# x normed by features on GpSimd from a second copy, another order of VectorE, and a last batch ended in halves

## The chip, the cores and the metric

One core of a Trainium2 chip runs the program. The metric is device microseconds of one execution, the median of the runs of a kernel. The engines are TensorE (PE in the profile; PEld is its weight load), VectorE (DVE), ScalarE (ACT), GpSimd (POOL) and SyncE (SP, which here only issues DMAs).

## The reference

For each of 16 batches of 512 tokens with 128 features:

```
n   = gamma * x / |x| * sqrt(128)                    # rms norm
q,k,v = n @ w_q * 0.25, n @ w_k, n @ w_v             # 8 heads of 16
phi(u) = [1, u, u_i * u_j / sqrt(2)]                 # second order Taylor features
att = phi(q) @ (phi(k)^T v) / max(phi(q) . sum phi(k), 1e-5)
x1  = layernorm(x + att @ w_out)
h   = silu(x1 @ w1 * s1) * (x1 @ w2 * s2)            # 128 -> 512
h   = gelu(h @ h1 * hs1); h = gelu(h @ h2 * hs2)     # 512 -> 512, exact gelu
out = layernorm(x1 + h @ w3 * s3)                    # 512 -> 128
```

All is float32. The kernel keeps the accuracy by splitting each activation into a rounded high part (type fp32r) and the rest, and multiplying each by the weights.

## The kernel before

Every engine has its own program, written out by hand; semaphores order them. The work is a pipeline over batches in steps t = 0 to 18: step t does the FRONT of batch t (norm of x, projections, phi(k), state, sums for phi(q)), the MIDDLE of batch t - 1 (state applied to phi(q), attention, projection, x1), the FFN of batch t - 2 and the TAIL of batch t - 3 (last layer norm, store). Steps 0 and 1 are mostly written out by themselves, steps 3 to 14 run in a loop of two steps a turn, and steps 15 to 18 are peeled. `B` is 16, `P` 128, `N` 512, `NT` and `KT` 4.

PSUM is two sets of four banks. `RING` lists in PE's order what is written into the attention's four banks (`ring`), `FPS` the same for the feed-forward part (`fps`). A write waits until the reader of the bank's last content has released it (`bank_wait`, `ring_free`, `f_free`).

x comes once per batch, tokens on partitions, into one of two buffers `x_b` (SP L277). ACT squares it (`square`, L629), DVE sums the squares (`sum_squares`, L829, L833), POOL takes the power -0.5 (L1080) and scales x (L1085, tile `xn`), all in the step before the batch's FRONT. PE transposes `xn` (`transpose_x`, L309) into the ring; ACT copies it rounded (`x_hi`, L639) and DVE subtracts (`x_lo`, L844). Then PE projects k and v in four products of tokens (`project_kv`, L322) and q (`project_q`, L329). ACT copies k and v out (`copy_kv`, L633), DVE makes the products of k (`phi_k_main`, L257), POOL the small features (`k_small`, L1099 to L1108); `copy_q` and `q_lo` (L852, L856) split q. `sums_of_q` and `rest_of_q` (L348, L355) make sums that ACT squares (`square_sums`, L660; `square_rest`). `state` (L368) is 64 small products. In the next step the state is transposed (L378, L385) and applied (L398, L407), `normalise` divides on DVE, `project_out` (L415) projects, and DVE adds x (`sum_x1`, L889), takes the variance and scales (`norm_scale`, L882); PE transposes x1 (L423), and ACT and DVE split it (L670, `x1_lo` L923).

The feed-forward products are pairs, high (L431) and low part (L434). `silu`, `gate_mult`, `gate_hi`, `gate_lo` (L696, L930, L701, L936) make the gate. `gelu` on ACT writes the rounded part (L709) and the exact one over the bank (L711), and `gelu_tile` on DVE (L944) subtracts. `copy_y` (L716), `transpose_y` (L476), `sum_z` (L907), POOL's power (L1122), `norm_scale` into `o_b` and the store (L282) end a batch.

`keep_busy` (L586) is a product on ones whose result nobody reads. `weights_low_bits` (L680) finds whether the weights have low bits that rounding would lose; after step 1 PE branches on the result.

## Time and profile before

| | |
|---|---|
| median of 3 runs | 564.23 us (562.71 to 565.49) |
| the profiled execution | 565.74 us, its span 563.9 us |
| busy share PE, DVE, ACT, POOL | 97%, 81%, 82%, 28% |
| share of the chain that ended last | PE 89%, issue 4%, ACT 2%, DVE 2% |
| products of the feed-forward part (L431, L434) in that chain | 28% and 27% |

Times in the rows are us from the start of the span. A busy PE row can hold pipelined products: starts tell more than durations. The granted clock of PE (PEclk) has two levels here, 1.2 and 2.4 GHz, 0.5 and 1.0 in the rows. The idle time in brackets is what came before the operation on its engine, with what ended it.

### The profile page before, as it was taken

What the parts mean: (1) busy time and instruction counts of PE and PEld (TensorE: products, weight loads), DVE (VectorE), ACT (ScalarE), POOL (GpSimd) and SP (SyncE); (2) the same over time, 40 slices, a digit from 0 to 9 for tenths busy, and PEclk for the clock granted to TensorE, in tenths of its full rate; (3) what the DMA queues carried; (4) which work ended last, traced back from release to release, by engine and by line L of the source; (5) the groups of instructions that cost most, each with busy time, mean ns of one, the idle gap of its engine ahead of it and who ended that gap; (6) DMA issues with size and microseconds to landing.
All of it is one profiled execution on the core that took longest, in us unless ns stands there. A gap on an engine that the chain in (4) does not pass through costs nothing.

```text
span 563.9 us, 11483 instructions
## 1 busy us (share of the span) xinstructions
PE 545.4 (97%) x3608; PEld 410.3 (73%) x3608; DVE 457.1 (81%) x982; ACT 460.5 (82%) x954; POOL 159.5 (28%) x246
## 2 busy tenths in 40 slices
PE   7879999999999999999999999999999999999994
PEld 3446877878687787868778786877878787786772
DVE  5776769888787988878798887879888787968764
ACT  4757797988979798897979889797988979787773
POOL 3541414223151422314142222414222241400000
PEclk9799999999999999999999999999999999999998
DMA  8000000000000000000000000000100000000000
GB/s 274 18 22 2 19 2 2 20 19 20 20 19 19 0 19 19 19 19 19 19 0 19 18 19 19 19 19 0 29 8 19 19 19 19 1 19 1 20 1 37
DMA packets 7366, 12.25 MB, mean 22 GB/s; under 512 B 816, under 2 KB 1840, under 8 KB 7344
## 3 DMA queue, kind: packets, MB, share of 16 engines
q1 hardware_dynamic: 7056, 11.86, 6.6%
q8 instruction: 13, 0.21, 0.2%
q10 hardware_dynamic: 288, 0.10, 0.1%
q14 instruction: 9, 0.07, 0.0%
HBM read 7.77 MB, written 4.19 MB: 21 GB/s over the span
## 4 chain that ended last, share of the span: by engine, by line
PE 89%; issue 4%; ACT 2%; DVE 2%; POOL 1%; DMA 1%; SPq 0%; POOLq 0%; DVEq 0%
PE fps L431 28%; PE fps L434 27%; PE ring L368 7%; PE ring L398 5%; PE ring L348 5%; PE ring L322 4%; PE ring L407 3%; PE ring L415 2%; PE ring L329 2%; PE fps L476 1%; PE fps L423 1%; PE ring L309 1%; PE ring L355 1%; DMA w_raw<-in_w 1%; PE ring L378 1%
## 5 line engine op out<-in xcount | busy, mean ns | idle before, releaser
L431 PE MATMUL fps<-hid_hi,w_hi 128*128 128x512 f32 x576 | 229.7, 399 | 0.0
L434 PE MATMUL fps<-hid_lo,w_hi 128*128 128x512 f32 x576 | 226.9, 394 | 1.3 <-DVE hid_lo L944 0.9
L709 ACT ACTIVATE hid_hi<-fps,col 128x512 fp32r<-128x512 f32 x128 | 90.3, 705 | 54.1 <-PE fps L434 54.1
L431 PEld LDWEIGHTS fps<-hid_hi,w_hi 128*128 128x128 f32 x576 | 108.3, 188 | 25.4 <-issue 3.4
L434 PEld LDWEIGHTS fps<-hid_lo,w_hi 128*128 128x128 f32 x576 | 108.3, 188 | 25.0 <-DVE hid_lo L944 2.2
L944 DVE TENSOR_TENSOR hid_lo<-fps,hid_hi 128x512 fp32r<-128x512 f32 x128 | 88.2, 690 | 32.4 <-ACT fps L711 30.8
L711 ACT ACTIVATE fps<-fps,col 128x512 f32<-128x512 f32 x128 | 86.6, 677 | 0.0
L660 ACT ACTIVATE phiT<-ring 128x512 f32<-128x512 f32 x127 | 77.2, 636 | 5.1 <-PE ring L348 4.0
L930 DVE SCALAR_TENSOR_TENSOR h<-fps,col,gate_zo 128x512 f32<-128x512 f32 x64 | 47.8, 748 | 38.7 <-ACT gate_zo L696 34.5
L257 DVE TENSOR_TENSOR phi_k<-phi_k 128x896 f32<-128x896 f32 x64 | 69.1, 1085 | 0.2 <-ACT v_one L633 0.2
L348 PE MATMUL ring<-qT,sel 128*128 128x512 f32 x128 | 52.9, 417 | 3.5 <-ACT v_one L633 2.0
L431 PE MATMUL fps<-x1T_hi,w_hi 128*128 128x512 f32 x128 | 52.5, 411 | 1.5 <-DVE x1T_lo L923 1.5
L1099 POOL TENSOR_TENSOR k_half<-v_one,const 128x16 f32<-128x16 f32 x32 | 14.6, 456 | 130.4 <-ACT v_one L633 128.7
L434 PE MATMUL fps<-x1T_lo,w_hi 128*128 128x512 f32 x128 | 51.0, 398 | 0.0
L701 ACT ACTIVATE hid_hi<-h 128x512 fp32r<-128x512 f32 x64 | 42.8, 668 | 9.1 <-DVE h L930 9.1
L1080 POOL TENSOR_TENSOR rn<-ssc,const 128x4 f32<-128x4 f32 x16 | 16.3, 1016 | 116.0 <-DVE ssc L833 115.8
L696 ACT ACTIVATE gate_zo<-fps,col 128x512 f32<-128x512 f32 x64 | 45.9, 717 | 1.9 <-PE fps L434 1.8
L936 DVE TENSOR_TENSOR hid_lo<-h,hid_hi 128x512 fp32r<-128x512 f32 x64 | 43.8, 684 | 1.8 <-ACT hid_hi L701 0.2
L689 ACT ACT_TABLE_LOAD x33 | 42.3, 1283 | 2.2 <-PEq L1187 1.7
L368 PE MATMUL ring<-phi_k,v_one 128*32 128x153 f32 x1024 | 38.6, 305 | 0.4 <-ACT phiT L660 0.4
L368 PEld LDWEIGHTS ring<-phi_k,v_one 128*32 128x32 f32 x1024 | 32.6, 114 | 7.2 <-issue 4.8
L1122 POOL TENSOR_TENSOR zrstd<-zveps,const 128x4 f32<-128x4 f32 x16 | 16.1, 1009 | 70.2 <-DVE zveps L918 70.2
(100 smaller groups left out, 902.3 us busy)
## 6 DMA issues: line engine op xcount, KB each, us to landing
x_b<-in_x SPq DMA_DIRECT2D x16, 256.0 KB, 2.6
out<-gate_zo SPq DMA_DIRECT2D x16, 256.0 KB, 2.0
w_raw<-in_h SPq DMA_DIRECT2D x2, 1024.0 KB, 9.4
w_raw<-in_w SPq DMA_DIRECT2D x3, 256.0 KB, 4.6
sel_raw<-in_sel SPq DMA_DIRECT2D x1, 320.0 KB, 6.0
w_qkv_raw<-in_w_kv SPq DMA_DIRECT2D x1, 128.0 KB, 2.8
const<-in_consts ACTq DMA_DIRECT2D x1, 92.0 KB, 3.0
w_qkv_raw<-in_w_q SPq DMA_DIRECT2D x1, 64.0 KB, 2.8
```

Source lines behind the costliest of these rows:

```text
L257: return eng.tensor_tensor(out, fixed, moved, ALU.mult)
L348: nc.tensor.matmul(ring[:, bank_of(RING, f"sq{f}"), :], sel[:, l * P:(l + 1) * P], qT[g][:, :], start=True, stop=True).then_inc(ring_full, 1)
L368: mm = nc.tensor.matmul(ring[32 * hh:32 * hh + 32, bank, g * FEAT:(g + 1) * FEAT], v_one[:, j, 4 * g + hh, :], phi_k[:, j, 4 * g + hh, 0:F ...
L431: nc.tensor.matmul(fps[:, bank, :], w[:, o:o + P], hi, start=start, stop=False)
L434: return nc.tensor.matmul(fps[:, bank, :], w[:, o:o + P], lo, start=False, stop=stop)
L660: nc.scalar.activation(phiT[:, f, :], ring[:, bank, :], ACT.Square).then_inc(ring_free[bank], 1)
L696: nc.scalar.activation(gate[:, m % 2, :], fps[:, bank_of(FPS, f"a{m}"), :], ACT.Silu, scale=s1_c[:, m:m + 1]).then_inc(f_free[bank_of(FPS, ...
L709: nc.scalar.activation(hid[1 - layer][0][:, m, :], fps[:, bank, :], ACT.Gelu, scale=scale)\
L711: nc.scalar.activation(fps[:, bank, :], fps[:, bank, :], ACT.Gelu, scale=scale)\
L930: nc.vector.scalar_tensor_tensor(out=h32[:, m, :], in0=fps[:, bank_of(FPS, b), :], scalar=s2_c[:, m:m + 1], in1=gate[:, m % 2, :], op0=ALU ...
L936: nc.vector.tensor_tensor(hid[0][1][:, m, :], h32[:, m, :], hid[0][0][:, m, :].bitcast(F32), ALU.subtract).then_inc(split_ready, 1)
L944: nc.vector.tensor_tensor(lo, fps[:, bank, :], hi.bitcast(F32), ALU.subtract)\
```

## The change

The host hands over x twice, once as before and once with features first (`xT`). From step 2 on PE no longer transposes x. SP loads x by tokens (`x_nrm`) for the squares, x by features (`x_cols`) for the products, and x again for the residual (`x_res`). POOL's powers (`norm_of_x`) go as 512 numbers to DRAM (`rn_rows`) and come back as a row on every partition (`rn_row`, `spread_norms`). In the batch's own step POOL multiplies `x_cols` by it (`normed_cols`), ACT makes the rounded copy from that (`scaled_hi`), and POOL subtracts in DVE's place; PE waits for that (`x_lo_ready`). Batches 0 and 1 keep the transposes.

ACT squares the next batch's x ahead of the gelus of layer 2, not between those of layer 3. DVE sums the squares behind `sum_z`, splits `q_lo` around `sum_x1`, takes the variance (`var_of_x1`) behind the last gelu tile of layer 2 and makes all products of k after it.

At the start, `weights_low_bits(1)` goes behind the first step's squares; all but three of the sums of batch 1 move ahead of PE's branch; PE gets more `keep_busy`; the load of the silu table moves to step 2.

The last batch's fourth tile of layer 3, its y, its transposes, layer norm and store are done in halves of 256 tokens. Tokens j * 128 + p, not 4 * p + j, now lie on partition p of the residual and the output, so those rows in DRAM are 512 bytes long and not 2048.

```diff
+            def load_norm_parts(n):
+                sp.wait_ge(sq_ready, n)
+                sp.dma_start(x_nrm[:, :, :], x_d[bass.ds(n, 1)].rearrange("b p j d -> (b p) j d"))\
+                    .then_inc(nrm_loaded, 16)
...
+            def load_cols(n):
+                if is_positive(n - 2):
+                    sp.wait_ge(x_scaled_ready, n - 2)
+                sp.dma_start(x_cols[:, :], xT[bass.ds(n, 1)].rearrange("b d n -> (b d) n")).then_inc(cols_loaded, 16)
...
+            def spread_norms(n):
+                sp.wait_ge(rn_ready, n + 1)
+                sp.dma_start(rn_d, rn[:, :]).then_inc(rn_stored, 16)
+                sp.wait_ge(rn_stored, 16 * (n - 1))
+                sp.dma_start(rn_row[:, :], rn_all).then_inc(rn_row_loaded, 16)
...
+            def load_residual(n):
+                if is_positive(n):
+                    sp.wait_ge(ring_free[bank_of(RING, "out")], read(RING, n, "out"))
+                sp.dma_start(x_res[:, :, :], x_res_d[bass.ds(n, 1)].rearrange("b p j d -> (b p) j d"))\
+                    .then_inc(res_loaded, 16)
...
+                    if not is_step(t, 1):
+                        load_norm_parts(t + 1)
+                    load_cols(t + 1)
+                    if not is_step(t, 1):
+                        spread_norms(t + 1)
+                if front:
+                    load_residual(t)
+                if is_step(t, 1):
+                    spread_norms(2)
+                if is_step(t, B + 2):
+                    for half in range(2):
+                        js = slice(2 * half, 2 * half + 2)
+                        sp.wait_ge(z_scaled, half + 1)
+                        sp.dma_start(out_d[B - 1][:, js, :], o_b[:, js, :]).then_inc(stored, 16)
...
-            peeled(step, 0)
+            sp.dma_start(o_b[:, :, :], x_res_d[1]).then_inc(x1_nrm_loaded, 16)
...
+            load_residual(0)
             sp.dma_start(w_o[:, :], w_out).then_inc(w_out_loaded, 16)
+            sp.wait_ge(xn_ready, 1)
+            sp.dma_start(x_nrm[:, :, :], x_d[2]).then_inc(nrm_loaded, 16)
             peeled(step, 1)
             steps_from_2(sp, step)
-            sp.wait_ge(stored, 16 * B)
...
+                if j == 0 and not is_step(t, 0) and not is_step(t, 1):
+                    pe.wait_ge(x_lo_ready, t - 1)
...
+                if is_step(t, 0) and 2 <= f < 7 or is_step(t, 1) and 2 <= f < 5:
+                    keep_busy(P)
...
-                nc.tensor.matmul(fps[:, bank, :], w[:, o:o + P], hi, start=start, stop=False)
+                out = fps[:, bank, 0:hi.shape[1]]
+                nc.tensor.matmul(out, w[:, o:o + P], hi, start=start, stop=False)
                 if wait_lo is not None:
                     pe.wait_ge(*wait_lo)
-                return nc.tensor.matmul(fps[:, bank, :], w[:, o:o + P], lo, start=False, stop=stop)
+                return nc.tensor.matmul(out, w[:, o:o + P], lo, start=False, stop=stop)
             def layer1(t, m, in_full):
                 for what, o in ((f"a{m}", o1), (f"b{m}", o2)):
@@ -477,41 +549,67 @@
...
+            def last_layers(t, in_full):
...
+                    for k in range(KT):
+                        mm = product(bank, oh2 + k * HID + 3 * P, hid[1][0][:, k, cols], hid[1][1][:, k, cols], k == 0,
+                                     k == KT - 1, in_full)
+                    mm.then_inc(half_full, 1)
+                for half, cols in enumerate(HALVES):
+                    bank = Y_BANK[half]
+                    pe.wait_ge(f_free[bank], read(FPS, t, ("three1", "three2")[half]))
...
                     if is_step(t, 2):
                         for part in range(4):
                             pe.wait_ge(w_hi_ready[part], 1)
-                        sums_of_q(1, 0)
-                        sums_of_q(1, 1)
-                        rest_of_q(1, 0)
-                        sums_of_q(1, 2)
                         transpose_x1(1, 0)
+                        sums_of_q(1, 5)
+                        keep_busy(256, 3)
                     if ffn:
                         layer1(t, 0, in_full)
...
                     if is_step(t, 2):
-                        sums_of_q(1, 4)
-                        rest_of_q(1, 1)
-                        sums_of_q(1, 5)
                         sums_of_q(1, 6)
                         state(1)
                         sums_of_q(1, 7)
                     if middle:
                         transpose_state(t)
                         transpose_rest(t)
-                    if front:
-                        transpose_x(t)
+                    if is_step(t, 0):
+                        transpose_x(0)
...
+                    if is_step(t, B + 2):
+                        last_transposes()
+                    elif tail:
                         transpose_y(t)
...
+                    if is_step(t, 0):
+                        keep_busy(N)
...
+                    if is_step(t, B + 1):
+                        last_layers(t, in_full)
+                        return
...
-                for _ in range(4):
-                    keep_busy(N)
+                sums_of_q(1, 0)
+                sums_of_q(1, 1)
+                rest_of_q(1, 0)
+                for f in (2, 3, 4):
+                    sums_of_q(1, f)
+                rest_of_q(1, 1)
...
+            def scaled_hi(t):
+                act.wait_ge(x_scaled_ready, t - 1)
+                nc.scalar.activation(xnT_hi[:, :], x_scaled[:, :], ACT.Copy).then_inc(x_hi_ready, 1)
...
+            def last_gelu(t):
+                for half, cols in enumerate(HALVES):
+                    act.wait_ge(half_full, half + 1)
+                    bank = fps[:, THREE_BANK[half], 0:N // 2]
+                    nc.scalar.activation(hid[0][0][:, 3, cols], bank, ACT.Gelu, scale=hs2_c[:, 3:4])\
+                        .then_inc(half_hi_ready, 1)
+                    nc.scalar.activation(bank, bank, ACT.Gelu, scale=hs2_c[:, 3:4]).then_inc(half_gelu_ready, 1)
...
+            def last_copy():
+                for half, cols in enumerate(HALVES):
+                    act.wait_ge(y_full, half + 1)
+                    nc.scalar.activation(yT[:, cols], fps[:, Y_BANK[half], 0:N // 2], ACT.Copy, scale=s3_c)\
...
                 if is_step(t, 2):
-                    square_sums(1, 2)
+                    load_table(ACT.Silu)
                     silu(t, 0)
-                    square_sums(1, 3)
+                    square_sums(1, 5)
                     silu(t, 1)
-                    square(2, 0)
-                    square_sums(1, 4)
-                    square_rest(1, 1)
-                    square_sums(1, 5, 6)
+                    square_sums(1, 6)
...
+                if is_step(t, 0) or is_step(t, 1):
                     x_hi(t)
+                elif front:
+                    scaled_hi(t)
...
+                if ffn and front and not is_step(t, B - 1):
+                    square(t + 1)
...
                 if is_step(t, 1):
-                    load_table(ACT.Silu)
+                    square(2)
...
-                if is_step(t, 1):
-                    x1_hi(t)
-                elif front:
+                if front:
                     square_sums(t, 2)
                 if ffn:
                     gelu(t, 1, 1)
-                if front and not is_step(t, 1) and not is_step(t, B - 1):
-                    square(t + 1, 1 - par)
-                if front and not is_step(t, 1):
+                if is_step(t, 0):
+                    square(1)
+                if front:
...
-                if front and not is_step(t, 1):
...
+                if is_step(t, B + 1):
+                    last_gelu(t)
...
+                if is_step(t, 1):
+                    x1_hi(t)
+                elif front:
                     square_sums(t, 5)
...
+                    weights_low_bits(1)
...
-            square(0, 0)
-            weights_low_bits(1)
+            square(0)
...
+            def var_of_x1(t):
...
+            def last_lo():
+                for half, cols in enumerate(HALVES):
+                    dve.wait_ge(half_gelu_ready, half + 1)
...
+            def last_norm():
+                js = [slice(2 * half, 2 * half + 2) for half in range(2)]
+                for half in range(2):
+                    dve.wait_ge(yT_full, half + 1)
...
+                dve.wait_ge(stored, 16 * (B - 1))
+                for half in range(2):
+                    dve.wait_ge(z_rstd_ready, half + 1)
...
-                if is_step(t, 2):
-                    sum_squares(2)
-                if front:
-                    x_lo(t)
...
+                if front and not is_step(t, B - 1):
+                    sum_squares(t + 1)
                 if ffn:
                     gelu_tile(t, 0, 0)
-                if front:
-                    phi_k_main(t, 0)
-                if ffn:
                     gelu_tile(t, 0, 1)
                 if front:
-                    q_lo(t, 0, 1)
+                    q_lo(t, 0)
                 if ffn:
                     gelu_tile(t, 0, 2)
                 if middle:
-                    sum_x1(t, 1 - par)
+                    sum_x1(t)
+                if front:
+                    q_lo(t, 1)
                 if ffn:
                     gelu_tile(t, 0, 3)
-                if front:
+                if middle:
+                    var_of_x1(t)
+                if front:
+                    phi_k_main(t, 0)
                     phi_k_main(t, 1)
+                if is_step(t, B + 1):
+                    scale_z(t)
                 if ffn:
                     gelu_tile(t, 1, 0)
                 if middle:
@@ -994,14 +1177,12 @@
                     gelu_tile(t, 1, 2)
                 if middle:
                     x1_lo(t)
-                if front and not is_step(t, B - 1):
-                    sum_squares(t + 1)
-                if ffn:
+                if is_step(t, B + 1):
+                    last_lo()
+                elif ffn:
                     gelu_tile(t, 1, 3)
-                if tail:
-                    if is_positive(t - 3):
-                        dve.wait_ge(stored, 16 * (t - 3))
-                    norm_scale(t - 3, z, zmv, zrstd, zmv_ready, zrstd_ready, o_b, out_ready)
+                if tail and not is_step(t, B + 1):
+                    scale_z(t)
...
-                round_weights(dve, nc.vector, 0)
-                round_weights(dve, nc.vector, 1)
-                round_weights(dve, nc.vector, 2)
+                for part in range(4):
+                    round_weights(dve, nc.vector, part)
                 x_lo(1)
-                round_weights(dve, nc.vector, 3)
                 normalise(1)
...
+                q_lo(1, 0, 1)
+                sum_x1(1)
+                var_of_x1(1)
+                sum_squares(2)
+                norm_scale(0, x1p, mv, rstd, mv_ready, rstd_ready, x1[0], x1_ready)
                 phi_k_main(1, 0)
-                sum_x1(1, 0)
-                q_lo(1, 0)
-                norm_scale(0, x1p, mv, rstd, mv_ready, rstd_ready, x1[0], x1_ready)
-                q_lo(1, 1)
                 x1_lo(1)
                 phi_k_main(1, 1)
...
+            def norm_of_x(t):
                 pool.wait_ge(ssc_ready, t + 1)
+                if is_positive(t - 2):
+                    pool.wait_ge(rn_stored, 16 * (t - 2))
                 nc.gpsimd.tensor_tensor(rn[:, :], ssc[:, :], neg_half, ALU.pow).then_inc(rn_ready, 1)
...
+            def normed_cols(t):
+                pool.wait_ge(cols_loaded, 16 * (t - 1))
+                pool.wait_ge(rn_row_loaded, 16 * (t - 1))
+                nc.gpsimd.tensor_tensor(x_scaled[:, :], x_cols[:, :], rn_row[:, :], ALU.mult).then_inc(x_scaled_ready, 1)
+                pool.wait_ge(ring_full, written(RING, t - 1, "qT"))
+                pool.wait_ge(x_scaled_ready, t - 1)
+                pool.wait_ge(x_hi_ready, t + 1)
+                nc.gpsimd.tensor_tensor(xnT_lo[:, :], x_scaled[:, :], xnT_hi[:, :].bitcast(F32), ALU.subtract)\
+                    .then_inc(x_lo_ready, 1)
...
+                    normed_cols(t)
...
+                if is_step(t, B + 2):
+                    for half in range(2):
+                        js = slice(2 * half, 2 * half + 2)
...
+                if front and not is_step(t, B - 1):
+                    norm_of_x(t + 1)
                 if front:
                     k_small(t, 1)
                 if middle:
                     inv_std(t - 1, veps_ready, veps, rstd, rstd_ready)
-                if front and not is_step(t, B - 1):
-                    normed_x(t + 1, 1 - par)
...
-            normed_x(0, 0)
-            peeled(step, 0)
+            normed_x(0, x_nrm[:, :, :])
+            k_small(0, 0)
+            k_small(0, 1)
+            normed_x(1, o_b)
             spread_rest(1)
             k_small(1, 0)
             inv_std(0, veps_ready, veps, rstd, rstd_ready)
             pool.wait_ge(x1_ready, 1)
             k_small(1, 1)
-            normed_x(2, 0)
+            norm_of_x(2)
             steps_from_2(pool, step)
...
+    data["xT"] = _np.ascontiguousarray(data["x"].transpose(0, 2, 1))
```

## Rows read from the trace of the kernel before

**Rows 1.** Page, part 1 (busy us, share, instructions) and 2 (clock by slice).
```profile
PE 545.4 (97%) x3608; PEld 410.3 (73%) x3608; DVE 457.1 (81%) x982; ACT 460.5 (82%) x954; POOL 159.5 (28%) x246
...
PEclk9799999999999999999999999999999999999998
```

**Rows 2.** Timeline of PE, one middle step: start, us, engine, line, operation, count.
```profile
311.49 0.27 PE L385 MATMUL ring<-const,st_rest 128*128 128x128 f32 x1
311.60 0.60 PE L309 MATMUL ring<-const,xn 128*128 128x128 f32 x4
311.96 0.48 PE L431 MATMUL fps<-x1T_hi,w_hi 128*128 128x512 f32 x1
...
317.26 0.37 PE L322 MATMUL ring<-w_qkv_hi,xnT_hi 128*128 128x264 f32 x1
...
335.40 0.60 PE L423 MATMUL fps<-const,x 128*128 128x128 f32 x4
```

**Rows 3.** Chain that ended last, in order: start, us, what; two state products.
```profile
76.58 2.22 PE ring L368 x64
...
502.70 2.22 PE ring L368 x64
```

**Rows 4.** Timeline of ACT in the same step.
```profile
322.25 0.69 ACT L709 ACTIVATE hid_hi<-fps,col 128x512 fp32r<-128x512 f32 x1 [0.89 <-PE fps L434]
...
335.01 0.66 ACT L629 ACTIVATE sq<-x_b 128x512 f32<-128x512 f32 x1
```

**Rows 5.** Timeline of DVE in the same step.
```profile
313.32 0.69 DVE L844 TENSOR_TENSOR xnT_lo<-ring,xnT_hi 128x512 fp32r<-128x512 f32 x1 [0.27 <-ACT xnT_hi L639]
...
327.42 0.69 DVE L944 TENSOR_TENSOR hid_lo<-fps,hid_hi 128x512 fp32r<-128x512 f32 x1 [0.17 <-ACT fps L711]
...
333.55 1.11 DVE L882 TENSOR_SCALAR x<-x1p,mv,rstd 128x128 f32<-128x128 f32 x4
```

**Rows 6.** Timeline of POOL and DVE at that step's end, side by side.
```profile
340.06 1.83 DVE L882 TENSOR_SCALAR gate_zo<-gate_zo,zmv,zrstd 128x128 f32<-128x128 f32 x4
340.66 1.15 POOL L1085 TENSOR_TENSOR xn<-x_b,rn 128x512 f32<-128x512 f32 x1 [0.17 <-POOL rn L1080]
```

**Rows 7.** Windows: length, busy PE, PEld, DVE, ACT, POOL, clock, DMA share, GB/s.
```profile
13.00:15.00 2.00, 0.22 (x1) 0.00 (x0) 1.63 (x3) 1.70 (x5) 2.00 (x4) 1.00 0.89 325
19.60:24.00 4.40, 4.40 (x66) 3.07 (x65) 4.03 (x9) 2.28 (x4) 1.83 (x2) 0.51 0.01 4
41.00:44.40 3.40, 3.13 (x8) 2.49 (x9) 3.40 (x5) 1.29 (x2) 0.00 (x0) 0.50 0.00 0
```

**Rows 8.** Timeline of ACT in step 0, the check of the w3 weights.
```profile
8.17 0.63 ACT L680 ACTIVATE hid_lo<-w_raw 128x512 fp32r<-128x512 uint16 x1 [4.02 <-DMA w_raw<-in_w]
```

**Rows 9.** The same chain over the first steps.
```profile
19.71 4.28 PE ring L368 x64
...
38.07 0.70 DVE qT L856
...
41.27 0.77 PE fps L431
...
46.33 2.33 PE ring L368 x64
...
55.13 0.93 PE ring L322 x6
```

**Rows 10.** Timeline of PE and of DVE at the end.
```profile
554.84 0.51 PE L434 MATMUL fps<-hid_lo,w_hi 128*128 128x512 f32 x1 [0.46 <-DVE hid_lo L944]
...
556.89 0.69 DVE L907 TENSOR_TENSOR gate_zo<-x,fps 128x512 f32<-128x512 f32 x1 [1.08 <-PE fps L476]
...
560.36 1.12 DVE L882 TENSOR_SCALAR gate_zo<-gate_zo,zmv,zrstd 128x128 f32<-128x128 f32 x4 [1.22 <-POOL zrstd L1122]
```

**Rows 11.** DMA issues: what, queue, count, KB each, median us to landing.
```profile
x_b<-in_x SPq DMA_DIRECT2D x16, 256.0 KB, 2.6
out<-gate_zo SPq DMA_DIRECT2D x16, 256.0 KB, 2.0
```

149 lines of the change are left out of this document (113 added, 36 removed).

## The prediction

> **What bounds the kernel now.** I read the page first: TensorE (PE) is busy 97% of the span, VectorE (DVE) 81%, ScalarE (ACT) 82%, and the granted clock is below full only in the first slices and the last [rows 1]. Then the chain of waits: between the state products of one step and the same products thirteen steps later it is one unbroken run on PE, (502.70 - 76.58) / 13 = 32.78 us a step [rows 3]. Inside a step the PE timeline has the products starting one behind the other without a wait [rows 2]. So in the middle only PE's own instructions count, and everything on the other engines is free until it comes late for PE. At the start PE stands still or runs at half clock: in 13 to 15 us it has 0.22 us of work, in 19.6 to 24 and in 41 to 44.4 the granted clock is 0.51 and 0.50 [rows 7]. The end is a chain over four engines without other work beside it [rows 10].
>
> **Part 1, the middle: the transposes of x go.** In a step PE starts the transpose of the state's rest at 311.49, the four of x at 311.60 and the next product at 311.96 [rows 2]. The change drops the four in steps 2 to 15, 14 times. 311.96 - 311.60 = 0.36 us, and the switch of data type that follows them follows the other transpose just as well, so 0.36 stays as the price; 14 x 0.36 = 5.0 us. The upper bound takes the 0.11 us that lie between the first two starts for each of the four: 0.44, 6.2 us. The lower bound is nothing, if another engine takes over the bound.
>
> Now what replaces them, queue by queue, in the frame of this step, where PE comes 0.36 us earlier than before.
> - ScalarE: the rounded copy stays in its place, from SBUF. The square leaves 335.01, where the engine has no gap, for the gap of 0.89 us ahead of 322.25 [rows 4]. With PE 0.36 earlier that gap is 0.53, and the square has 0.66: it hides, and the late half of the step gains some 0.6 us of room.
> - VectorE loses x_lo (0.69 at 313.32), takes the sum of squares and its scaling (0.9 us) early, behind sum_z, and moves the products of k down behind the variance. Its first queue is late by those 0.9 us, but at 327.42 it stood waiting for ScalarE's gelu, itself released by PE; that comes at 327.06 now. From there I count, from the starts of the same operations in VectorE's timeline: gelu_tile 0.61, sum_x1 0.7, second q_lo 0.7, gelu_tile 0.6, variance 2.1, two products of k 2.0, gelu_tile 0.6, which puts norm_scale at 333.8 and x1_ready at 334.9 (it starts at 333.55 now). PE will ask for x1 at 335.40 - 0.36 = 335.04 [rows 2, 5]. That is the tightest place: a slack of 0.74 shrinks to about 0.1 to 0.2.
> - GpSimd (POOL) gets two 128x512 operations in place of one of 1.15 [rows 6]. x_lo there comes after ScalarE's rounding and ends near 314.2 (VectorE's starts at 313.32 now [rows 5]); PE's first projection needs it at 317.26 - 0.36 = 316.9 [rows 2]. VectorE's gate work is what it can disturb. The rows show such disturbance: norm_scale of four parts takes 1.83 us beside POOL's 1.15 us operation and 1.12 alone [rows 6, 10], 0.7 more. Laid on gate_lo that is 0 to 0.7 us on the first queue, and the wait ahead of 327.42 absorbs it. I take nothing.
> - SyncE: norms go out to DRAM and come back as a row. A load lands in 2.6 us, a store in 2.0 [rows 11]; 4.6 us for the pair, against some 15 us from the norm of the next batch to its use in the next step. The residual load behind it and the output store behind that have as much room. Nothing.
>
> The Trainium skill, "SBUF — State Buffer", section "SBUF: two separate sides", says that GpSimd and VectorE take a shared port pair as an exclusive lock when the VectorE operation has two SBUF inputs, the loser waiting for the whole instruction. The trace agrees with such holding in size, 0.7 us beside a 1.15 us operation [rows 6, 10]. By the rule gate_lo(0) would wait about 0.6 us in each step; the sum stays if the wait at 327.42 is still there, and would be 14 x 0.6 = 8.4 us worse if it were not.
>
> **Part 2, the start.** (a) ScalarE's check of the w3 weights stood 4.0 us waiting for their load, then took 0.6 us and its read-out, ahead of x_hi [rows 8]; moved behind, x_hi follows the transposes at once: -0.5 us. The work comes back as 0.7 us ahead of the first state's copy. (b) Extra products fill PE after project_q and between the sums. If they hold the clock, the first state products take 2.2 us as in the middle and not 4.28 [rows 3, 9]: -2.1. With (a) that is 2.6, less the 0.7: -1.9 at the copy of the state. The price if not: 2.1 of it stays. (c) In step 1 the second q_lo (0.70, between norm_scale and the transposes of x1 [rows 9]) leaves that place, and the sums that PE had queued ahead of the transposes are done earlier: -0.9 at the first product of layer 1 (41.27). (d) Those sums are done before step 2 begins, so state(1) follows two pairs of layer-1 products. Before, it started at 46.33, 5.1 us after layer 1 began [rows 9], of which 3.4 at half clock [rows 7]; now 8 products of 0.23 and one sum, about 2.1, then some 0.5 for VectorE's last products of k: -2.5. Together -5.3. (e) The new wait: in step 2 the norms of x must go through DRAM, and they start only after k_small(1, 1). By my count rn is ready near 41.8, plus 4.6 is 46.4, plus 1.15, 0.65 and 1.15 for scaling, rounding and x_lo is 49.4; PE would reach kv(2) at 55.13 - 5.3 - 0.4 = 49.4 [rows 9, 11]. So the wait is met about evenly; ScalarE's queue behind scaled_hi (gate_hi, silu 2 and 3) is held, and PE may stand 0.4 to 0.8 in layer 2. I book +0.7. Each us that the round trip takes over 4.6 adds one. Start: -4.6 us, bounds -1.5 (both clock falls stay) and -5.6.
>
> **Part 3, the end.** From the last product's wait (0.46 us at 554.84) to the last scaling's end at 561.48 [rows 10]. In halves of 256 columns, which I price at two thirds of a full instruction (fixed part included), half A's y is ready some 0.75 us earlier than now (554.6 for 555.35); copy 0.45, transposes 0.45; then VectorE is the chain: 1.4 for sum, statistics and epsilon of each half (2.3 for the whole now), to 558.3; the power on POOL 1.05, the scaling of two parts 0.6: 559.95. 561.48 - 559.95 = 1.5 us. The store of half B is smaller than the one now but has shorter rows: nothing to +0.3 less. I take -1.6; bounds -0.7 and -2.2, as halves cost three quarters or six tenths.
>
> **Sum.** -5.0 - 4.6 - 1.6 = -11.2 us. The profiled execution is 565.74 (span 563.9), the median of the runs shown is 564.23. 565.74 - 11.2 = 554.5 us for an execution like the profiled one, and the same saving from the median gives **553.0 us**.
>
> **Rivals.**
> - The clock falls again in one or both places of the start. For it: the sums are still paced by ScalarE, and about 1 us without work remains ahead of the first sum. Against: the 2 us hole becomes half of it. The saving at the start is 1.5 to 3: 555.5 us.
> - x1 comes late for PE in each step, the 0.1 to 0.2 us of slack turning into a wait of 0.3 us: 13 x 0.3 = 3.9, so 557 us. For it: my count adds seven durations read to 0.05 us. Against: each of them is read next to its neighbour in the same engine's rows.
> - The change doesn't shorten the step at all, ScalarE or VectorE holding 32.8 us: 553.0 + 5.0 = 558 us. Against: 82% and 81% busy [rows 1].
> - Slower than before. The place is norm_scale of x1 on VectorE, now behind the variance, two products of k and a gelu tile. If these and POOL's locks make x1 over 0.9 us late in each step (11.2 / 13 is the point from which it decides), the gain is gone; at 1.1 us the time is 553.0 + 14.3 = 567.5. It would need some 1.1 us over my count; only the 0.7 of rows 6 is in sight, and it lies ahead of a wait.
>
> **How the numbers follow.** Forecast 0.55, the clock 0.2, x1 late 0.12, no shorter step 0.08, slower 0.03, the rest (gains over the bounds) 0.02. Forecast, clock and x1 late hold 0.87; to 558.5 nearly all of the fourth comes in. On the low side the bounds give 5.6 + 6.2 + 2.2 = 14.0, unlikely together; I end the range at 550.5, so 550.5 to 558.5. About 0.5% (2.8 us) is what a measurement here can tell from no change: faster by more 0.95, within 0.02, slower by more 0.03.
>
> **What would show it.** The chain of waits between state products one step apart: 32.42 us instead of 32.78, and no wait of PE for x1. Granted clock 1.00 from 17 to 45 us, and state products of 2.2 us at the start. The first projection of step 2 near 49.5 to 50 instead of 55.13, released by POOL's x_lo. At the end 5.2 us or less from the last product of y to the end of the last scaling, where it is 561.48 - 555.35 = 6.1 now. The prediction is wrong if PE waits for VectorE or POOL in the middle, if the norms' round trip is well over 4.6 us, or if the clock falls at the start.

## The result, and the profile after

The median fell from 564.23 to 559.67 us (five runs each, 558.59 to 560.52 after; ratio 0.9913, 95% interval 0.9886 to 0.994): 4.6 us where 11.2 were forecast, and outside the range. The profiled execution took 560.52 us with a span of 557.0; before it was 565.74 with 563.9. The span lost 6.9 us, and the time around it grew from 1.8 to 3.5 us.

The page after, parts 1 and 2 (columns as in [rows 1]):

```profile
PE 537.5 (96%) x3580; PEld 404.3 (73%) x3580; DVE 452.2 (81%) x971; ACT 463.5 (83%) x957; POOL 177.8 (32%) x261
PEclk9997999999999999999999999999999999999998
```

The shares hardly moved. The fourth slice (41.8 to 55.7 us) still has a reduced clock. Busy time by stretch, the same three stretches as [rows 7] (busy us and instructions of each engine, then granted clock, DMA share, GB/s):

```profile
13.00:15.00 2.00, 1.43 (x5) 0.51 (x3) 1.62 (x3) 1.37 (x4) 2.00 (x4) 1.00 1.06 372
19.60:24.00 4.40, 3.48 (x70) 2.55 (x68) 4.21 (x10) 4.25 (x10) 2.60 (x4) 1.00 0.02 4
41.00:44.40 3.40, 2.73 (x7) 1.82 (x6) 3.07 (x4) 2.79 (x5) 0.93 (x1) 0.50 0.02 1
```

The first fall of the clock is gone, the second is there. The chain of waits (start, us, what) from the scaling of x1 to the state products of batch 1, then the chain at the state products of the next two steps and of the last one, beside [rows 3, 9]:

```profile
36.85 1.13 DVE x L1020 x4
37.98 2.06 issue
40.04 0.64 PE fps L494 x4
40.70 0.61 ACT x1T_hi L788
41.33 0.70 DVE x1T_lo L1070
42.17 0.76 PE fps L503
...
46.34 3.02 PE ring L439 x64
...
76.83 2.22 PE ring L439 x64
...
109.27 2.22 PE ring L439 x64
...
497.99 2.22 PE ring L439 x64
```

(`issue` in the chain is time in which PE waited for nothing that the profile shows.) This splits the difference. Up to the state products of the second loop step the kernel is at 76.83 us; before it was at 76.58: **the start gained nothing, +0.25**. Thirteen steps take 421.16 us, 32.40 each in place of 32.78: **the middle gained 4.96**. From the last state products to the span's end it is 557.0 - 497.99 = 59.0, before 563.9 - 502.70 = 61.2: **the end gained 2.2**.

Three places more. PE's timeline ahead of x1's transposes (start, us, engine, line; idle time before it and what ended it), POOL's in step 2, and what waits in the middle (total, times, longest):

```profile
35.58 0.47 PE L426 MATMUL ring<-qT,sel 128*128 128x512 f32 x1
40.04 0.63 PE L494 MATMUL fps<-const,x 128*128 128x128 f32 x4 [3.98 <-issue]
```

```profile
40.92 1.01 POOL L1262 TENSOR_TENSOR rn<-ssc,const 128x4 f32<-128x4 f32 x1
49.89 0.39 POOL L1309 TENSOR_TENSOR st_rest<-st,const 128x100 f32<-128x100 f32 x1 [7.96 <-ACT st L747]
50.24 1.29 POOL L1277 TENSOR_TENSOR x_scaled<-x_cols,rn_row 128x512 f32<-128x512 f32 x1
52.37 1.28 POOL L1281 TENSOR_TENSOR xnT_lo<-x_scaled,xnT_hi 128x512 fp32r<-128x512 f32 x1 [0.83 <-ACT xnT_hi L757]
```

```profile
PEld fps L494 <- DVE x L1020: 3.3, 13, 0.3
```

x1 was ready at 37.98, but PE went on at 40.04: it stood for 3.98 us ("issue") with nothing to wait for that the profile shows. Between these two instructions the program has the load of the low bits' sum into a register and the branch to one of two copies of the loop. In the kernel before, four products of 512 columns stood ahead of that branch; the change put the sums there.

### The profile page after: what moved, and what is told of

The parts are those of the page before. It is cut to its first block, busy times and chain, and to the rows that moved or that the text cites. A ratio compares the mean times of both kernels' runs of the same rounds, so it can differ in the third digit from the quotient of the medians.

```text
span 557.0 us, 11623 instructions
## 1 busy us (share of the span) xinstructions
PE 537.5 (96%) x3580; PEld 404.3 (73%) x3580; DVE 452.2 (81%) x971; ACT 463.5 (83%) x957; POOL 177.8 (32%) x261
## 4 chain that ended last, share of the span: by engine, by line
PE 90%; issue 1%; DVE 1%; ACT 1%; POOL 1%; POOLq 0%; DVEq 0%
PE fps L503 29%; PE fps L506 29%; PE ring L439 6%; PE ring L469 5%; PE ring L417 5%; PE ring L391 4%; PE ring L478 3%; PE ring L486 2%; PE ring L398 2%; PE fps L548 1%; PE fps L494 1%; PE ring L426 1%; PE ring L449 1%; DVE h L1077 1%; PE ring L456 0%
## 5 line engine op out<-in xcount | busy, mean ns | idle before, releaser
L503 PE MATMUL fps<-hid_hi,w_hi 128*128 128x512 f32 (+1 forms) x584 | 230.7, 396 | 0.0
L506 PE MATMUL fps<-hid_lo,w_hi 128*128 128x512 f32 (+1 forms) x584 | 227.3, 390 | 0.9 <-DVE hid_lo L1091 0.5
L503 PEld LDWEIGHTS fps<-hid_hi,w_hi 128*128 128x128 f32 x584 | 109.8, 188 | 26.5 <-issue 3.4
L506 PEld LDWEIGHTS fps<-hid_lo,w_hi 128*128 128x128 f32 x584 | 109.8, 188 | 22.9 <-DVE hid_lo L1091 0.9
L1091 DVE TENSOR_TENSOR hid_lo<-fps,hid_hi 128x512 fp32r<-128x512 f32 x127 | 85.7, 684 | 11.8 <-ACT fps L829 11.0
L1083 DVE TENSOR_TENSOR hid_lo<-h,hid_hi 128x512 fp32r<-128x512 f32 x64 | 53.9, 842 | 18.5 <-ACT hid_hi L819 16.8
L819 ACT ACTIVATE hid_hi<-h 128x512 fp32r<-128x512 f32 x64 | 41.4, 647 | 16.6 <-DVE h L1077 16.6
L1309 POOL TENSOR_TENSOR st_rest<-st,const 128x100 f32<-128x100 f32 x16 | 6.6, 411 | 133.1 <-ACT st L747 133.1
L1317 POOL TENSOR_TENSOR rstd<-veps,const 128x4 f32<-128x4 f32 x16 | 27.3, 1705 | 51.1 <-DVE veps L1042 51.1
L439 PE MATMUL ring<-phi_k,v_one 128*32 128x153 f32 x1024 | 37.3, 298 | 0.0
```

Source lines behind the costliest of these rows:

```text
L439: mm = nc.tensor.matmul(ring[32 * hh:32 * hh + 32, bank, g * FEAT:(g + 1) * FEAT], v_one[:, j, 4 * g + hh, :], phi_k[:, j, 4 * g + hh, 0:F ...
L503: nc.tensor.matmul(out, w[:, o:o + P], hi, start=start, stop=False)
L506: return nc.tensor.matmul(out, w[:, o:o + P], lo, start=False, stop=stop)
L1083: nc.vector.tensor_tensor(hid[0][1][:, m, :], h32[:, m, :], hid[0][0][:, m, :].bitcast(F32), ALU.subtract).then_inc(split_ready, 1)
L1091: nc.vector.tensor_tensor(lo, fps[:, bank, :], hi.bitcast(F32), ALU.subtract)\
```

## The experiments

Each kernel was timed beside the kernel before on the same chip, in four sittings. The median of the kernel before in them was 563.84, 563.5, 564.8 and 565.19 us, and its 50 runs went from 562.1 to 568.0; where two kernels come from different sittings, their ratios to it are the fairer comparison. **The changed kernel again** gives the yardstick.

> The changed kernel itself, as the yardstick of the other kernels on this chip. All theories expect what its first runs showed: median 559.7 us against 564.2 of the kernel before (-4.5), state products of the second loop step at 76.8 us, 32.4 us a step from there on, and about 2 to 3.5 us of time outside the span.

559.52 us (557.69 to 560.59). In this profiled execution the clock was low only until 43.9 us, the state products of batch 1 began at 45.18, and the span was 555.3: how long the clock stays down differs from execution to execution.

**Without load and branch.**

```
-            lo_bits = pe.value_load(lo_sum[:, :].bitcast(mybir.dt.int32))
-            with pe.If(lo_bits != 0):
-                steps_from_2(pe, steps_with(True))
-            with pe.Else():
-                steps_from_2(pe, steps_with(False))
+            steps_from_2(pe, steps_with(False))
```

> TensorE no longer loads the sum of the low bits into a register and branches on it; it runs the copy of the loop for weights without low bits at once (the other copy is left out, so for other weights the result would be less exact). THEORY A (the hole: in the changed kernel the load and the branch take 4.4 us behind the last sum, nothing covers them, and the clock falls behind them): the transposes of x1 start at 38.0 us instead of 40.04, the clock stays at 1.00 from 17 to 50 us, layer 1 starts near 40.0 instead of 42.17. The state products then end near 44.3 instead of 49.3. How much of that arrives depends on the norms: if their way through DRAM takes 7 us, as measured, kv(2) starts near 52.2 instead of 55.3 (-3.1, total near 556.6); if it doesn't bind, near 50 (-5.3, total near 554.4). RIVAL B (the order on VectorE and ScalarE, not the branch, holds the start): the transposes come early but kv(2) stays within 0.7 us of 55.3, total within 1 us of the changed kernel's.

559.47 us (558.36 to 560.87): no gain, where theory A had 556.6 or less. The hole did go, x1's transposes start at 38.47 and the state products at 42.85. Then (POOL's and PE's timeline, and two stretches):

```profile
42.14 1.85 POOL L1258 TENSOR_TENSOR rn<-ssc,const 128x4 f32<-128x4 f32 x1
46.26 0.40 POOL L1305 TENSOR_TENSOR st_rest<-st,const 128x100 f32<-128x100 f32 x1 [2.27 <-ACT st L743]
49.89 1.28 POOL L1273 TENSOR_TENSOR x_scaled<-x_cols,rn_row 128x512 f32<-128x512 f32 x1 [3.23 <-DMA rn_row<-rn_rows]
```

```profile
53.32 0.39 PE L391 MATMUL ring<-w_qkv_hi,xnT_hi 128*128 128x264 f32 x1 [1.58 <-POOL xnT_lo L1277]
```

```profile
48.00:52.00 4.00, 3.74 (x28) 1.00 (x26) 0.00 (x0) 0.80 (x2) 1.28 (x1) 1.00 0.36 114
52.00:58.00 6.00, 4.46 (x17) 3.17 (x18) 5.52 (x8) 4.87 (x13) 1.83 (x4) 0.77 0.15 44
```

The norms' way through DRAM is the next bound: POOL waits 3.23 us for the row, PE 1.58 for x_lo, and behind that wait the clock falls again (0.77 between 52 and 58). What the branch had cost is lost again in full: the next state products start at 77.14, in the changed kernel at 76.83. The power itself took 1.85 us here beside VectorE's products of k, not 1.01.

**The early norm, with and without the branch.** GpSimd's norm of batch 2 goes ahead of its wait for x1:

```
+            norm_of_x(2)
             pool.wait_ge(x1_ready, 1)
             k_small(1, 1)
-            norm_of_x(2)
```

> The changed kernel, branch and all, with the norm of batch 2 computed before GpSimd waits for x1. It completes the square of two causes: both there 559.5, branch gone alone 559.5, both gone 555.6. THEORY (two bounds, one behind the other: the hole puts the state products at 46.3 or 45.2, and x_scaled then follows the state's copy, not the row): the early norm alone gains nothing, 559.5 within 0.7, with the transposes of x1 at 40.0 and the clock falling as in the changed kernel. RIVAL (the norms' way is half of the loss by itself): 557.5.

559.35 us (558.79 to 560.24). PE's transposes at 40.31, its state products at 46.55.

> As the kernel without the branch, and GpSimd computes the norm of batch 2 before it waits for x1 and before the second k_small of batch 1 (about 36.3 us instead of 40.9). THEORY N (without the branch the norms' way through DRAM is the next bound of step 2): rn is ready near 37.3 instead of 41.9, x_scaled no longer waits for the row, kv(2) starts near 50 instead of 52.2, total 2 us under the kernel without the branch alone. RIVAL: the norms had been in time there too: no difference over 0.5 us between the two, and GpSimd's k_small 1 us later at the worst.

555.59 us (555.32 to 556.64), ratio 0.9847 (0.9814 to 0.9879); first projections at 51.52 us and no wait ahead of them, clock 1.00 from 13 us on. The square: both causes 559.5, without the branch 559.5, early norm 559.4, both 555.6. Either cure alone gives nothing, both together 3.9 us, twice the 2 us that theory N had for the early norm.

**The hole's two costs apart.** Four products of 512 columns behind the last sum and ahead of the branch.

```
                 rest_of_q(1, 1)
+                for _ in range(4):
+                    keep_busy(N)
```

> The changed kernel with four extra products of 512 columns queued on TensorE behind the last sum and ahead of the branch: they keep TensorE at work while the branch is resolved but don't make it shorter. THEORY A, with the hole's two costs apart: the transposes of x1 stay near 40.0 to 40.3 us (2.0 us late), but the clock stays at 1.00 between 41 and 47.6, so layer 1 of four products takes 1.9 instead of 3.5 us and the state products 2.2 instead of 3.0: state(1) ends near 46.5 instead of 49.3, kv(2) near 52.3 to 53, total 2.3 to 3.0 under the changed kernel's. RIVAL C (the clock falls for another reason than the hole, for instance the wait for VectorE's x1_lo): the clock is 0.5 there again and the total is that of the changed kernel, or up to 1 us more.

557.39 us (556.96 to 558.28), 2.1 less, where 2.3 to 3.0 were expected. (`keep_busy(N)` shows as two records; four of them are the x8 below.) PE (timeline), and the same stretch as above:

```profile
35.89 3.60 PE L690 MATMUL fps<-v_one 128*128 128x512 f32 x8
40.18 0.63 PE L494 MATMUL fps<-const,x 128*128 128x128 f32 x4 [0.69 <-issue]
```

```profile
41.00:44.40 3.40, 2.56 (x12) 1.68 (x10) 2.93 (x4) 3.28 (x6) 0.94 (x1) 1.00 0.02 1
```

The transposes stay where they were, the clock holds, layer 1's first product starts at 42.31 and the state products at 44.55. So the clock's fall is worth about 2 us, and the hole's own 2 us of lateness stay. Here the state products come early enough to meet the norms' row again: POOL waits 0.23 us for it, 6.1 us after the norm was ready (48.04 for 41.93).

**Load or branch.** In the first kernel the load moves up behind `project_out`, the branch stays; in the second the load stays and the branch goes. Both have the early norm.

```
+            def load_sum():
+                pe.wait_ge(lo_sum_ready, 1)
+                return pe.value_load(lo_sum[:, :].bitcast(mybir.dt.int32))
...
                 project_out(1)
+                loaded = load_sum()
                 sums_of_q(1, 0)
...
-            second_step()
-            pe.wait_ge(lo_sum_ready, 1)
-            lo_bits = pe.value_load(lo_sum[:, :].bitcast(mybir.dt.int32))
+            lo_bits = second_step()
```

```
             lo_bits = pe.value_load(lo_sum[:, :].bitcast(mybir.dt.int32))
-            with pe.If(lo_bits != 0):
-                steps_from_2(pe, steps_with(True))
-            with pe.Else():
-                steps_from_2(pe, steps_with(False))
+            steps_from_2(pe, steps_with(False))
```

> The changed kernel with the early norm, and TensorE's load of the sum into a register moved up behind project_out, ahead of the sums; the branch stays behind the last sum. The 4.4 us from the last sum to the transposes of x1 are two things, the load and the branch. THEORY L (the load is most of it, over 2.4 us): the transposes start at 38.2 to 38.4 us, held by norm_scale alone, total near 555.8; the first sum may come later by what the load takes beyond project_out. THEORY J (the branch and the fetch of the code behind it are most of it; the instruction queue moves two packets between 37 and 38 us): the transposes start at 39.5 to 40.0 as now, the clock falls behind them, total near 559.

> The changed kernel with the early norm; the load of the sum stays where it is, the branch goes (one copy of the loop follows). THEORY L: the transposes start 2.4 to 4.4 us behind the last sum's start (38.3 to 40.0), later than with neither. THEORY J: they start at 38.3, held by norm_scale as with neither load nor branch, total near 555.6.

558.39 us (557.64 to 561.48) and 556.05 (555.14 to 558.08). The last sum and the transposes of each, first the one with the load ahead, then the one without the branch:

```profile
36.75 0.48 PE L426 MATMUL ring<-qT,sel 128*128 128x512 f32 x1
40.72 1.08 PE L494 MATMUL fps<-const,x 128*128 128x128 f32 x4 [3.50 <-issue]
```

```profile
36.88 0.48 PE L426 MATMUL ring<-qT,sel 128*128 128x512 f32 x1
39.42 0.81 PE L494 MATMUL fps<-const,x 128*128 128x128 f32 x4 [2.06 <-DVE x L1017]
```

With the load gone from there 3.97 us remain from the last sum to the transposes; in the three profiles with both in place it is 4.36 (the changed kernel again), 4.46 (its first profile) and 4.73 (early norm alone). Without the branch it is 2.54, and PE waits for VectorE alone. It is the branch, theory J, and the load is 0.4 to 0.8 us of it, from one profile. Both profiles here are later from the start on (first sum at 33.55 and 33.69 where the early norm alone has 32.35), since in both the clock was low between 13 and 16 us (0.57 and 0.53), which the profiles of the changed kernel and of the early norm alone don't show.

What the branch waits for is less sure. The Trainium skill, "Runtime: NRT & Kernel Launch", section "Instruction fetch mechanics", says that a taken branch to code outside the window already fetched waits for a DMA to bring the page. The trace agrees as far as it goes. In the changed kernel two packets move on the instruction queues between 37 and 38 us, in the hole. The one on q14 comes between 34 and 40 us in the four kernels without the branch too (the next one included); the one on q8 comes in each kernel that has the branch (between 36 and 39 us) and in none of the four without it between 34 and 42. That it is the fetch that takes the 4 us is argued from this, not shown. The Trainium skill's "Advanced Engine Details and Errata", section "Control Flow Timing", gives a compare-and-branch some 0.1 us; for this branch the measured 4 us decide.

**The branch in the kernel before.**

```
-            with pe.If(lo_bits != 0):
-                steps_from_2(pe, steps_with(True))
-            with pe.Else():
-                steps_from_2(pe, steps_with(False))
+            steps_from_2(pe, steps_with(False))
```

> The kernel before, without TensorE's load of the sum into a register and without the branch (only the loop for weights without low bits is left). THEORY A (there the branch was free, since four products of 512 columns queued ahead of it keep TensorE at work to 36.88 us while it is resolved): the first sum of step 2 starts at 36.7 as before, everything behind it stays, total within 0.5 us of the kernel before. RIVAL: the branch costs its 4.4 us wherever it stands (the sums start earlier and the total falls by 1 us or more).

565.3 us (562.4 to 565.99) beside 563.5, ratio 1.002 (1.0004 to 1.0036): no gain, if anything a loss of 1 us where 0.5 at most was expected, which stays unexplained. From project_out to the first sum behind the filling it is 34.45 - 30.07 = 4.38 us, with the branch 36.70 - 32.31 = 4.39. There the branch was free. In this profiled execution the first state products took 2.29 us (4.31 in the other), with no filling ahead of them: the first fall of the clock isn't in every execution of this code.

**The sums put back behind the branch,** as before, in the changed kernel: `project_out`, four `keep_busy(N)`, branch, four sums, one `keep_busy(N)`, x1's transposes, the other sums around layer 1. The small filling between the sums of batch 1 goes, and ScalarE's order matches the new one.

```
                 project_out(1)
+                for _ in range(4):
+                    keep_busy(N)
-                sums_of_q(1, 0)
-                sums_of_q(1, 1)
-                rest_of_q(1, 0)
-                for f in (2, 3, 4):
-                    sums_of_q(1, f)
-                rest_of_q(1, 1)
...
+                        sums_of_q(1, 0)
+                        sums_of_q(1, 1)
+                        rest_of_q(1, 0)
+                        sums_of_q(1, 2)
+                        keep_busy(N)
                         transpose_x1(1, 0)
-                        sums_of_q(1, 5)
-                        keep_busy(256, 3)
+                        sums_of_q(1, 3)
+                        keep_busy(N, 3)
```

> The changed kernel with the branch kept, but put back behind project_out and four products of 512 columns; all sums of batch 1 come behind it: the first four ahead of the transposes of x1, one behind them, two after the first pair of layer 1, two after the second, with one product of 512 columns before and one after the transposes as filling. THEORY A with N: the transposes start near 38.0 to 38.3, the clock stays up, the state products end near 45.5, but the row of the norms lands only near 49.9, as without the branch; the first projections of step 2 start near 53.3 after a wait of TensorE for GpSimd's x_lo, total 559.5, no gain over the changed kernel. RIVAL: the norms' wait goes away with the branch's place (it was the extra lock of GpSimd by VectorE there): first projections near 51.5, total near 555.6.

> The kernel with the sums behind the branch, and the norm of batch 2 computed before GpSimd waits for x1. THEORY A with N (branch hole and norms are the two bounds that follow each other, and both must go): state products end near 45.5, the row of the norms lands near 44, first projections of step 2 near 51.5 as in the kernel without the branch with the early norm, total 555.6 (-4.0 against the changed kernel, -8.2 against the kernel before), now with the branch in it. RIVAL: sums so late hold ScalarE and VectorE back in layer 1: the state products come 1 to 2 us later, total 557.

559.16 us (558.69 to 559.91), and with the early norm 555.85 (555.53 to 556.56, ratio 0.9864, 0.9841 to 0.9888). In the first POOL waits 3.37 us for the row and takes x_scaled at 50.23; in the second x_scaled comes at 46.51, behind the state's copy. So both causes can be removed with the branch in place, and here the early norm alone is worth 3.3 us. PE of the first, whose clock stayed at 1.00 between 52 and 58:

```profile
53.66 0.39 PE L391 MATMUL ring<-w_qkv_hi,xnT_hi 128*128 128x264 f32 x1 [1.70 <-POOL xnT_lo L1287]
56.73 0.51 PE L506 MATMUL fps<-hid_lo,w_hi 128*128 128x512 f32 x1 [0.42 <-DVE hid_lo L1089]
```

The first projections are 2.1 us later than in the second (53.66 for 51.58), the q projection behind them 3.65 (60.51 for 56.86), and the next state products 3.66 (76.78 for 73.12). The other 1.6 us are lost at full clock in layer 2, whose gate tiles come late behind `scaled_hi`.

**Two steps further on that kernel.** VectorE's second q_lo moves behind `sum_squares(2)`; then the filling ahead of x1's transposes shrinks from 512 to 128 columns.

```
-                q_lo(1, 0, 1)
+                q_lo(1, 0)
...
                 sum_squares(2)
+                q_lo(1, 1)
```

```
                         sums_of_q(1, 2)
-                        keep_busy(N)
+                        keep_busy(P)
                         transpose_x1(1, 0)
```

> As the kernel with sums behind the branch and the early norm, and in step 1 VectorE does the second q_lo (0.69 us) not ahead of the sum of x1 but behind the sum of squares, in the 0.83 us in which it waits for GpSimd's inverse deviation. THEORY V (VectorE's chain to the last product of k sets the state products of batch 1: from the attention's end to 43.9 us it stands still only in that wait): norm_scale starts 0.6 to 0.7 earlier, the state products end that much earlier, total 0.6 us under the kernel with q_lo in its place. RIVAL: another engine sets it; no difference over 0.3 us.

> The kernel with the second q_lo later (555.65 us), with the filling product ahead of the transposes of x1 cut from 512 to 128 columns. There the transposes started at 38.39 us although x1 was ready near 37.8, behind the filling. THEORY (the filling took what the earlier x1 gave): the transposes start near 37.9, layer 1 and the state products 0.4 to 0.5 us earlier if the clock holds, total 555.2. RIVAL: VectorE's products of k set the state products anyway, or the clock falls without the filling: no gain, or 1 to 2 us more.

555.65 us (555.21 to 555.89): x1 was scaled 0.26 us earlier, not 0.6, since VectorE now waited 0.50 for project_out, and PE's filling took the rest (transposes at 38.39). With the smaller filling 555.27 (555.04 to 557.05), ratio 0.9844 (0.982 to 0.9868), transposes at 38.03. The two steps are worth 0.6 us between them (1.1 by the ratios), no more than the runs of one kernel differ; this is the fastest version.

**Step 0 without its filling,** on the 555.85 us kernel.

```
-                if is_step(t, 0) and 2 <= f < 7:
-                    keep_busy(P)
...
                         project_q(t)
-                    if is_step(t, 0):
-                        keep_busy(N)
```

> The kernel with the sums behind the branch and the early norm (555.85 us), less the extra products that the change puts into step 0 (one of 512 columns behind project_q, five of 128 between the sums). THEORY (the forecast's step 2 (b)): the clock falls again near 19.6 to 24 us, the first state products take about 4.3 instead of 2.3 us, the total rises by 2.1 us to 558.0. RIVAL: the clock stays up without them, because the first state's products come closer behind the sums now (no change, within 0.4 us); or it falls in some executions only, and these spread over 1.5 us or more where the filled kernel's spread over 1.

559.89 us (558.77 to 562.46): 4.0 more, or 3.4 by the ratios (0.9925 for 0.9864), well over the forecast 2.1. PE's timeline:

```profile
20.24 4.31 PE L437 MATMUL ring<-phi_k,v_one 128*32 128x153 f32 x64
...
37.82 0.70 PE L417 MATMUL ring<-qT,sel 128*128 128x512 f32 x2
40.43 0.39 PE L424 MATMUL ring<-qT,sel 128*128 128x512 f32 x1 [1.91 <-issue]
```

The clock (0.50 between 19.6 and 24) costs 2.0 in the state products, as the sum had it. The other 1.9 are a second "issue" hole, two instructions behind the branch, that no other profile here has. A packet on instruction queue q8 falls between 38 and 39 us, in that hole; whether it was late by chance or by the shifted addresses is open. The rival came true in part: one of the six executions kept its clock (0.998) and has the shortest span, 555.8, still 2.3 over the filled kernel's 553.5.

**The end in whole tiles,** on the same kernel; the same on each engine for `last_gelu`, `last_copy`, `last_lo`, `last_norm`, the powers and the stores.

```
-                    if is_step(t, B + 1):
-                        last_layers(t, in_full)
-                        return
...
-                    if is_step(t, B + 2):
-                        last_transposes()
-                    elif tail:
+                    if tail:
                         transpose_y(t)
```

> The same kernel with the last batch's end done in whole tiles of 512 tokens again, as in the kernel before (last layer, its rounding, copy, transposes, sum, statistics, store); only the early scaling of the batch before it stays. THEORY (trace of the changed kernel: from its last state products to the span's end 59.0 us where before had 61.2): the end is 2.2 us longer, total 558.0. The forecast had booked 1.6: 557.4. RIVAL: the earlier scaling of the batch before last and the one load less before the last store brought part of it: 1.2 us or less, total 557.0 or under.

558.00 us (557.83 to 558.26), 2.15 more, but only 1.1 by the ratios (0.9883 for 0.9864), so the median alone doesn't tell theory from rival. The traces do: from the last state products to the span's end it is 556.4 - 495.16 = 61.2 us, with halves 553.5 - 494.44 = 59.1.

**VectorE's old order in the loop,** on the same kernel.

```
                     gelu_tile(t, 0, 0)
+                    phi_k_main(t, 0)
                     gelu_tile(t, 0, 1)
-                    q_lo(t, 0)
+                    q_lo(t, 0, 1)
                     gelu_tile(t, 0, 2)
                     sum_x1(t)
-                    q_lo(t, 1)
+                    var_of_x1(t)
                     gelu_tile(t, 0, 3)
-                    var_of_x1(t)
-                    phi_k_main(t, 0)
                     phi_k_main(t, 1)
```

> The same kernel with VectorE's order of the kernel before in the loop for the products of k (the first ahead of the second gelu tile, the second behind the fourth), both q_lo together, and the statistics of x1 right behind its sum; the sum of squares stays early. THEORY (the forecast: the order keeps x1 in time with a slack of 0.1 to 0.2 us, and VectorE's total load is the same either way): in the old order the first product of k holds the gelu tiles and both q_lo hold sum_x1 by some 1.1 us, TensorE waits for hid_lo in layer 3 or for the first sums, and the step grows by 0.2 to 0.6 us: 3 to 8 us in all, 559 to 564. RIVAL: VectorE has room enough (82% busy) and the order doesn't matter: within 0.5 us of 555.85.

577.0 us (575.62 to 577.39), ratio 1.0219 (1.0197 to 1.0242), 20 to 21 us more. The step is (514.28 - 73.13) / 13 = 33.93 us, 1.5 longer, not 0.2 to 0.6. The chain of one step:

```profile
333.35 0.66 ACT fps L834
334.02 0.69 DVE hid_lo L1097
334.72 0.61 DVE x1p L1034
335.35 0.29 DVE stats L1042
...
336.80 0.70 DVE hid_lo L1097
337.55 0.50 PE fps L506
```

VectorE is the chain for 3.5 us, from 334.02 to 337.5: PE waits first for q_lo ahead of the first sum (0.68 us), then for the bank that sum_x1 frees, then for the gelu tile that stands behind the statistics. Which of the three moves that this edit takes back costs most isn't separated.

## Why the prediction was wrong, and where it was right

**The middle, right.** 32.40 us a step was measured, 32.42 forecast; 0.38 in place of 0.36 for the four transposes of x. Norm_scale of x1 starts at 331.48 and PE's transposes at 332.70, and PEld's wait for it is 0.3 us at the longest, 3.3 in thirteen steps, all beside the products that are still running. The hold that I laid on gate_lo is there:

```profile
310.88 1.28 POOL L1281 TENSOR_TENSOR xnT_lo<-x_scaled,xnT_hi 128x512 fp32r<-128x512 f32 x1 [2.00 <-ACT xnT_hi L757]
...
311.27 1.45 DVE L1083 TENSOR_TENSOR hid_lo<-h,hid_hi 128x512 fp32r<-128x512 f32 x1 [0.82 <-ACT hid_hi L819]
```

1.45 us where the next gate_lo takes 0.68. It was absorbed, but used up the room: VectorE shows no idle time from 311.27 to the scaling of x1, and reaches the gelu tile from which my count ran at 324.77, 7.93 us ahead of PE's transposes where the forecast had 7.98. The count itself has a slip: its seven durations add up to 7.3 us and not to the 6.7 that lie between 327.06 and 333.8, because the variance is put at 2.1. It takes 1.45 (327.42 to 328.87), so the 333.8 was right and the term was not; with the terms as written x1 would have been 0.4 late. POOL's two operations took 1.29 each, not 1.15, which nothing waited for. What I treated as mere regrouping, VectorE's order, turned out to carry 20 us: with the sum of squares moved forward, statistics and products of k had to move back. The second and third rival (x1 late, no shorter step) did not occur.

**The start, wrong, by 4.85 us: -4.6 forecast, +0.25 measured.** What it had wrong is step (c), in which the branch has no price, then the round trip in (e), sized at 4.6 us for 5.9 to 6.1. With the branch and the late norm both gone (profile of the kernel without branch and with the early norm), the state products of the second loop step start at 73.07, 3.5 earlier than before. So 3.8 of the 4.85 us are these two causes together, and 1.1 are terms of the sum that were too large. By its steps:
- (a) and (b): -1.9 forecast at the state's copy. The clock held (1.00 in 19.6 to 24) and the first state products took 2.29 us, so the 2.1 were there. But the copy of the state, which (b) has 1.9 earlier, is 1.0 earlier (22.98 for 24.02). The 0.5 of (a) was lost on the way: x_hi starts at 8.26 for 8.79, but x_hi and x_lo of the first batch write and read strided tiles now and take 1.08 and 1.07 us, where they took 0.58 and 0.69 (and take 0.60 and 0.68 in step 1, on plain tiles), so the first projection starts 0.34 later. PE's timeline, before and then after:

```profile
10.15 0.39 PE L322 MATMUL ring<-w_qkv_hi,xnT_hi 128*128 128x264 f32 x1 [1.02 <-DVE xnT_lo L844]
```

```profile
10.49 0.39 PE L391 MATMUL ring<-w_qkv_hi,xnT_hi 128*128 128x264 f32 x1 [1.47 <-DVE xnT_lo L982]
```

  The state products begin at 19.92 for 19.64, end 1.7 earlier, and then the copy waits for ScalarE's moved check (22.98 for an end of 22.14, the 0.8 that was counted as 0.7). The first projections of step 1 moved by 0.85, from 28.63 to 27.79. A term mis-sized by 0.9 to 1.1. Nor is the clock sure to hold at the start: in the profiles of three of the kernels built on the changed one it was low between 13 and 16 us (0.50 to 0.57).
- (c) -0.9 at layer 1: the step that failed. It says that the sums that PE had queued ahead of the transposes are done earlier, and never names what they moved past: the branch. The prediction goes queue by queue for the other engines, but not for PE's own. The branch's 4 us, free under four filling products, came out behind the last sum, 2.06 us of it on the chain. The 0.9 itself was too much as well: without the branch and with the early norm layer 1 starts at 40.45 for 41.27, of which 0.63 came with the projections of step 1 (28.00 for 28.63), so 0.2 is left for (c). x1 was ready at 38.05 before and at 38.18 there: VectorE's new order scales it no earlier.
- The rival "the clock falls again" had the event (0.50 in 41 to 44.4) but not the cause. It had a saving of 1.5 to 3 us at the start and 555.5 in all; the fall alone cost 2.1 (filled hole), on top of the lateness.
- (d) right in mechanism: in the kernel without branch and with the early norm state(1) comes 2.2 us after layer 1 begins (42.69 for 40.45), where it was 5.1.
- (e) the round trip: rn ready at 41.93, forecast 41.8, right. 4.6 us were taken for the pair, from a load of wide rows and the final store [rows 11]; without the branch it was 49.89 - 43.99 = 5.9 us from rn to the row's use, 6.1 with the hole filled (the row's load alone lands in 4.5 by the median), and rn was 1.7 later because two operations of GpSimd took longer beside VectorE's products of k (1.60 for 0.74 in k_small's last one, 1.85 for 1.01 in the power). The first projections came 1.8 later than with the early norm (53.32 for 51.52), and the next state products 4.1 later (77.14 for 73.07). The 2.3 between are mostly the layer 2 that the forecast put at 0.4 to 0.8: the kernel with the sums behind the branch loses 1.6 us there at full clock. At most some 0.7 us is left for the clock's fall behind that wait, which no term had.

Why neither error shows alone: the hole put the state products so late that the row had landed, and where the hole went, the row was late by as much. A sum of terms does not show that; a second pass through the start with each term put in might have.

**The end, right in mechanism.** -2.2 measured against -1.6, at the bound that I had given. An instruction of 256 columns costs 0.42 of VectorE against 0.69, and POOL's power for two columns 0.70 to 0.74 against 1.01, which I had left whole. The working gave 1.5 and 1.6 was booked, which changes nothing. The last scaling ends 5.08 us after the end of the last product of y (554.81 - 549.73), where the forecast had 5.2 or less and before it was 6.1:

```profile
549.45 0.28 PE L506 MATMUL fps<-hid_lo,w_hi 128*128 128x256 f32 x1
```

```profile
554.21 0.60 DVE L1121 TENSOR_SCALAR gate_zo<-gate_zo,zmv,zrstd 128x128 f32<-128x128 f32 x2 [0.33 <-POOL zrstd L1329]
```

**From the sum to the median.** Two further terms lay outside the sum. The time around the span was 1.8 to 1.9 us in all runs of the kernel before and 2.0 to 3.5 in the changed kernel's eleven, 2.6 by the median: 0.8 us, whose cause stays open. And the profiled execution of before was one with much low clock at the start (granted 0.987, span 563.9); five others of its executions have 0.996 or 0.997 and spans of 560.3 to 560.9. I took a clock fall off a median that holds it only in part. The fastest version's span, 553.2, is within 0.5 us of the 563.9 - 11.2 = 552.7 that the sum stood for; its median is still 2.3 us over the forecast. That agreement is in part luck, since this version has changes that the forecast didn't price. (The price of the last rival also has a slip: 553.0 + 14.3 is 567.3.)
